# Softmax sums of an attention block: summed and inverted by token on VectorE, turned back by TensorE, scaled out of PSUM on VectorE

## What is computed

```python
scores = jnp.einsum('bqhd,bkhd->bhqk', q, k) / scale      # layer 0 is causal, layer 1 is not
attn = jax.nn.softmax(scores, axis=-1)
out = jnp.einsum('bhqk,bkhd->bqhd', attn, v).reshape(b, s, H * HS)
return out @ W_proj + b_proj
```

## Time and profile before

| what | value |
|---|---|
| median of 3 runs | 792.87 us (792.82 to 799.92) |
| span of the profiled execution, first to last instruction | 785.0 us |
| granted TensorE clock over the span, as a share of full | 0.926 |
| PE busy | 648.3 us, 83% |
| PEld busy | 409.1 us, 52% |
| DVE busy | 533.8 us, 68% |
| ACT busy | 312.7 us, 40% |
| POOL busy | 212.5 us, 27% |

### The profile page before, as it was taken

The page is one execution under the profiler, slowest core; times in us unless marked ns, Lnnn a source line. Parts: engine busy times, 40 slices in busy tenths (PEclk is TensorE's granted clock), DMA queues, the critical chain, the costliest instruction groups (busy, mean ns, idle before and its releaser), DMA issues. The chain is left out here.

```text
span 785.0 us, 9221 instructions
## 1 busy us (share of the span) xinstructions
PE 648.3 (83%) x3406; PEld 409.1 (52%) x3406; DVE 533.8 (68%) x938; ACT 312.7 (40%) x580; POOL 212.5 (27%) x184
## 2 busy tenths in 40 slices
PE   5789677958867889878798879778798899898897
PEld 2234245424323665645265656545266567767597
DVE  2879637769997486668997486668997355543311
ACT  2334112424541325645552325735552324473141
POOL 4559530313562110032443110122543111001100
PEclk8999976979999899999899999989899999999999
DMA  6376910467770002484750002484740000000000
GB/s 123 43 182 157 307 48 1 49 171 167 180 170 1 11 1 24 91 219 110 177 119 10 10 0 26 105 201 108 175 120 10 1 1 2 1 1 11 1 1 10
DMA packets 26642, 61.70 MB, mean 79 GB/s; under 512 B 4928, under 2 KB 12752, under 8 KB 26608
## 3 DMA queue, kind: packets, MB, share of 16 engines
q1 hardware_dynamic: 26608, 61.26, 33.6%
HBM read 53.52 MB, written 3.54 MB: 73 GB/s over the span
## 5 line engine op out<-in xcount | busy, mean ns | idle before, releaser
L1969 POOL TENSOR_TENSOR state<-state,C_rows 128x1024 f32<-128x1024 f32 x42 | 109.6, 2610 | 146.9 <-DVE state L1477 101.4
L1009 PE MATMUL py<-state,sel 128*96 128x512 f32 x168 | 93.2, 688 | 30.6 <-POOL state L1969 30.4
L1082 PE MATMUL pd<-w_dn,act 128*128 128x192 f32 x480 | 85.1, 330 | 3.9 <-ACT act L1849 3.0
L1082 PEld LDWEIGHTS pd<-w_dn,act 128*128 128x128 f32 x480 | 78.6, 191 | 9.4 <-ACT act L1849 4.3
L1009 PEld LDWEIGHTS py<-state,sel 128*96 128x96 f32 x168 | 27.6, 179 | 73.8 <-POOL state L1969 40.3
L1477 DVE TENSOR_TENSOR_SCAN state<-decay,dx_rows 128x512 f32<-128x512 f32 x48 | 64.3, 1380 | 0.8
L919 PE MATMUL py<-identb 128*32 128x512 bf16 x220 | 63.6, 419 | 0.0
L1849 ACT ACTIVATE act<-pu,b_up 128x256 f32<-128x256 f32 x90 | 37.8, 471 | 62.8 <-PE pu L1070 62.4
L1066 PE MATMUL pu<-fT,w_up 128*128 128x256 f32 x180 | 58.3, 406 | 3.7 <-ACT act L1849 3.7
L2018 POOL TENSOR_TENSOR cT<-cT,inv_den 128x256 f32<-128x256 f32 x24 | 18.5, 771 | 144.7 <-DVE inv_den L1694 144.7
L1819 ACT ACTIVATE decay<-d_rows,a_neg 128x255 f32<-128x255 f32 x96 | 40.8, 498 | 29.0 <-DMA d_rows<-delta_dram 28.9
(11 more groups left out here) (298 smaller groups left out, 1288.4 us busy)
## 6 DMA issues: line engine op xcount, KB each, us to landing
dx_rows<-delta_x_dram SPq DMA_DIRECT2D x41, 512.0 KB, 5.1
d_rows<-delta_dram SPq DMA_DIRECT2D x36, 512.0 KB, 6.4
d_rows<-delta_x_dram SPq DMA_DIRECT2D x6, 512.0 KB, 5.2
w_dn<-exp_w_dram SPq DMA_DIRECT2D x1, 2304.0 KB
B_rows<-xdbl SPq DMA_DIRECT2D x4, 512.0 KB, 7.0
C_rows<-xdbl SPq DMA_DIRECT2D x4, 512.0 KB, 10.6
delta_x_dram<-delta_x SPq DMA_DIRECT2D x4, 384.0 KB, 3.4
w_up<-exp_w_dram SPq DMA_DIRECT2D x1, 1536.0 KB
```

The source lines that it names most:

```text
L1009: mm = nc.tensor.matmul(py[0:INNER, :], sel[:, first:first + INNER], flat(states[g % held])[:, paths], start=False, stop=(g == GROUPS - 1) ...
L1082: mm = nc.tensor.matmul(pd[:, WIDTH * tl:WIDTH * (tl + 1)], act[e % 2][:, m, 128 * tl:128 * (tl + 1)], w_dn[:, e, m, :], start=(m == 0), s ...
L1969: nc.gpsimd.tensor_tensor(now, now, C_rows[:, :], ALU.mult).then_inc(sc_done, 1)
```

## The change

The sums are taken by token, inverted as 8 numbers a partition, copied and turned back.

- `sums(ht)` on TensorE stands where `spread(ht)` stood. For each of the two token tiles, `cT[:, ht, 128 tokens]` is the stationary operand and `den_sel[:, :, 0]` (4 columns) the moving one, so that partition = token and column = head.
- `invert_sums(ht)` on VectorE inverts those 128x8 numbers into `inv_tok`, waits for that, and copies each number 32 times into `inv_den` (128x256).
- `spread(ht)` on TensorE turns `inv_den` back with two transposes. It waits for `den_inv`. For ht 0 and 1 it takes the place that `context(2)` and `context(4)` had, and these two move behind `shifted(3)` and `shifted(5)`. They now wait for `ctx_done`.
- `scale_context(ht)` on VectorE multiplies `cT` by `pm[:, 256:512]` in place, after `shift(3)`, after `shift(5)`, and at the end of the layer. GpSimd's `context_scale` is gone.
- A slot "summed" stands between "context" and "spread". No table puts work in it, so in the tail nothing is issued between `sums(2)` and `spread(2)`, and what stands in "spread" comes behind `spread(2)`.

```diff
-SLOTS = [(l, s) for l in range(2) for s in ("turned", "projected", *range(2 * UNITS), "context", "spread",
+SLOTS = [(l, s) for l in range(2) for s in ("turned", "projected", *range(2 * UNITS), "context", "summed",
+                                            "spread",
                                             "output")]
...
                             if u in (2, 4):
-                                pe.wait_ge(den_inv[l], u // 2)
+                                pe.wait_ge(ctx_done[l], u // 2)
...
+                        def sums(ht):
+                            pe.wait_ge(ctx_copied[l], ht + 1)
+                            if ht:
+                                pe.wait_ge(ctx_done[l], ht)
+                            for tl in range(TILES):
+                                mm = nc.tensor.matmul(pm[:, TOKENS + QUAD * tl:TOKENS + QUAD * (tl + 1)],
+                                                      cT[:, ht, 128 * tl:128 * (tl + 1)], den_sel[:, :, 0],
+                                                      start=True, stop=True)
+                            mm.then_inc(den_done[l], 1)
+
                         def spread(ht):
-                            pe.wait_ge(ctx_copied[l], ht + 1)
-                            nc.tensor.matmul(pm[:, TOKENS:2 * TOKENS],
-                                             den_sel[:, :, :].rearrange("p j i -> p (j i)"), cT[:, ht, :],
-                                             start=True, stop=True).then_inc(den_done[l], 1)
+                            pe.wait_ge(den_inv[l], ht + 1)
+                            for tl in range(TILES):
+                                mm = nc.tensor.transpose(pm[:, TOKENS + 128 * tl:TOKENS + 128 * (tl + 1)],
+                                                         inv_den[:, QUAD * tl:QUAD * (tl + 1), :].rearrange("p j i -> p (j i)"),
+                                                         ident[:, :])
+                            mm.then_inc(inv_spread[l], 1)
...
                             row_max(u)
-                            if u >= 1:
+                            if u in (3, 5):
+                                spread(u // 2 - 1)
+                            elif u:
                                 context(u - 1)
                             others((l, 2 * u))
                             shifted(u)
+                            if u in (3, 5):
+                                context(u - 1)
                             if u in (2, 4):
-                                spread(u // 2 - 1)
+                                sums(u // 2 - 1)
                             others((l, 2 * u + 1))
                         context(UNITS - 1)
                         others((l, "context"))
+                        sums(HTILES - 1)
+                        others((l, "summed"))
                         spread(HTILES - 1)
                         others((l, "spread"))
...
                         def invert_sums(ht):
                             dve.wait_ge(den_done[l], ht + 1)
-                            if ht:
-                                dve.wait_ge(ctx_done[l], ht)
-                            nc.vector.reciprocal(inv_den[:, :],
-                                                 pm[:, TOKENS:2 * TOKENS]).then_inc(den_inv[l], 1)
+                            link(nc.vector.reciprocal(inv_tok[:, :], pm[:, TOKENS:TOKENS + TILES * QUAD]))
+                            nc.vector.tensor_copy(inv_den[:, :, :], inv_tok[:, :].unsqueeze(2).to_broadcast(
+                                [128, TILES * QUAD, 2 * HEAD])).then_inc(den_inv[l], 1)
+
+                        def scale_context(ht):
+                            dve.wait_ge(inv_spread[l], ht + 1)
+                            nc.vector.tensor_tensor(cT[:, ht, :], cT[:, ht, :], pm[:, TOKENS:2 * TOKENS],
+                                                    ALU.mult).then_inc(ctx_done[l], 1)
...
                             if u in (2, 4):
                                 context_copy(u // 2 - 1)
+                            if u in (3, 5):
+                                scale_context(u // 2 - 1)
                             others((l, 2 * u))
...
                         invert_sums(HTILES - 1)
+                        others((l, "summed"))
+                        scale_context(HTILES - 1)
                         others((l, "spread"))
...
-                    def context_scale(l, ht):
-
-                        pool.wait_ge(den_inv[l], ht + 1)
-                        nc.gpsimd.tensor_tensor(cT[:, ht, :], cT[:, ht, :], inv_den[:, :],
-                                                ALU.mult).then_inc(ctx_done[l], 1)
-
                     for slot in SLOTS:
                         l, at = slot
-                        if run_a and at in (5, 9, "spread"):
-                            context_scale(l, {5: 0, 9: 1, "spread": 2}[at])
```

More of the change, by code:

```diff
@@ L494, in build @@
         probs = [sb(f"probs{i}", [128, 2, 2, TOKENS]) for i in range(2)]
-        inv_den = sb("inv_den", [128, TOKENS])
+        inv_tok = sb("inv_tok", [128, TILES * QUAD])
+        inv_den = sb("inv_den", [128, TILES * QUAD, HEAD * 2])
         cT = sb("cT", [128, HTILES, TOKENS])
@@ L616, in build @@
         den_inv = [isem(f"sums_inverted{i}") for i in range(2)]
+        inv_spread = [isem(f"inverses_spread{i}") for i in range(2)]
         den_done = [isem(f"sums_spread{i}") for i in range(2)]
```

## The result

The changed kernel takes 826.24 us (median of 4 runs, 821.58 to 831.25), the kernel before 795.62 us beside it: ratio 1.0416, 95% interval 1.0329 to 1.0503. It is slower by 4%, where 804.1 us (792 to 811) was predicted: the sign was right, the size was not.

What follows compares the result with a forecast made beforehand. TensorE's issue order was taken to set the time near the changed tiles, with VectorE counting only where a shift or tail waits. Unit and tail terms summed to +11.2 us: 792.87 + 11.2 = 804.1 us, range 792 to 811.

Steps and rivals of the forecast that it cites:

- The prices: Each new step per tile: reciprocal 0.20 us, copy 0.29, scaling 0.41, two transposes 0.31, sums about 0.5.
- the prediction's reading of the earlier trace: Layer 1: a copy at 0.29 us waits for a running times_C; one at 0.41 us does not.
- The sum: Unit and tail terms of all layers of FIRST, STEADY and LAST added up: +11.2 us in all.
- unit 5 of FIRST's layer 0: Other work fills the slot before shifted, so the cost is the transposes' 0.31 us alone; the sum books 0.6.
- a unit of LAST's layer 1: Nothing in the slot before shifted, so +0.57 us for each of both units; the sum books 0.4 and 0.6.
- The tails: Eight third tiles: TensorE waits inside the chain, 1.6 us from copy to filler against 0.6; +1.0 us where filler is on the path.
- Units 3 and 5: 16 tiles: shorter transposes replace context as cover for the shift; 6.3 us in all by the prediction's terms.
- `shifted(5)` of STEADY's layer 0: A sign in the changed trace: a hole of about 0.4 us before it.
- The clock: Rival: holes and transposes in the eight tails; the clock falls in four, 8 us more, 812 us; chance 0.12.
- the forecast's last sign: The prediction is wrong if the granted clock moves away from 0.926 by more than 0.01.
- The small loss: Rival: TensorE's filler swallows short delays; 798.5 us if half the terms vanish, 796 if only three tails remain; chance 0.36.
- VectorE as the bound: Rival: VectorE's order sets layer 1's units and tails; 13 us faster, 780 us; chance 0.12.

Runs made afterwards that it cites:

- tails_only: The changed kernel with only its tails (third tile of each layer, 8 of 24) new, the other 16 tiles as before; ratio 1.0223 to the kernel before.
- before_pad2: The kernel before with keep_busy matmuls issued as two of 256 columns, 24 in FIRST and all 33 of a STEADY pass; ratio 1.0111.
- before_order: The kernel before with only context(2) and context(4) moved behind shifted(3) and shifted(5); ratio 1.0160.
- before_again: The kernel before, unchanged, run once more for a second trace; 795.36 us.
- after_keep: The changed kernel with 13 more filler matmuls of 512 columns a STEADY pass, in slots 0 to 3 of layer 0; 814.51 us, ratio 1.0298.
- after_keep2: after_keep with three more filler matmuls in each tail of STEADY and LAST, between sums and the transposes; 810.26 us, ratio 1.0218 to the kernel before.
- before_keep: The kernel before with the same 13 filler matmuls in the same slots as after_keep; ratio 1.0012.
- the halves: Two kernels, each with part of the change: only the tails new (ratio 1.0223), or only units 3 and 5 new (ratio 1.0301).
- mm_spread: The changed kernel with the two transposes of the inverses issued as ordinary fp32 matmuls against the identity; ratio 1.0362 to the kernel before.
- before_pad: The kernel before with 26 keep_busy matmuls of a STEADY pass issued as two of 256 columns, FIRST unchanged; ratio 1.0044.
- before_pad3: The kernel before with all 33 keep_busy matmuls of a STEADY pass issued as two of 256 columns, FIRST unchanged; 791.32 us in its one run.

## Why the prediction was wrong

**The prices: right.** Reciprocal 0.20 us, copy 0.29, scaling 0.42, the two transposes 0.22 to 0.37 at full clock (0.22 at 308.00, 0.28 at 438.61) and 0.43 at a clock of 0.50 (496.65), `sums` 0.49 to issue (319.24 to 319.73). The copy is the one that waits for a running `times_C`: at 408.87 it takes 1.32 us and ends at 410.19, with the `times_C` of 407.69 ending 0.15 us before:

```profile
408.87 1.32 DVE L1715 COPY inv_den<-inv_tok 128x256 f32<-128x256 f32 x1
```
```profile
407.69 2.35 POOL L2000 TENSOR_TENSOR state<-state,C_rows 128x1024 f32<-128x1024 f32 x1 [3.54 <-DVE state L1499]
```

That is the prediction's reading of the earlier trace rows, now seen on a copy. The Trainium skill, "SBUF — State Buffer", section "Who interferes with whom", says that a VectorE instruction in a two-port mode and a GpSimd instruction shut each other out, the first one issued going first. The trace agrees with the wait (1.32 us instead of 0.29); that the copy runs in such a mode is not shown.

**The sum: two slips that cancel.** It books 0.6 us for unit 5 of FIRST's layer 0 and 0.4 for a unit of LAST's layer 1, where the list of cases gives 0.3 and 0.6; with these the 11.2 us are 11.0 to 11.1. And the 5.4 us that VectorE stood idle before its reciprocals don't say who waits for them; the rows on the waits do.

**The tails: right.** 1.58 us from the copy to the filler for 1.6, the hole of 0.63 for 0.6, and 5.9 us (3.4) in tails_only for the 4.9 of the sum.

**Units 3 and 5: mechanism right, size too small, by 4.1 us in one fit and within the error in the other.** The moved `context` costs 6.6 us (5.3) by itself and the transposes come on top: 10.4 (7.8) for 6.3. The prediction let the transposes cover part of what `context` had covered, site by site; together the sites gave less cover than that. `shifted(5)` of STEADY's layer 0 waited 0.24 us where 0.4 was forecast, so it isn't that hole; which sites make up the rest wasn't separated.

**The back edge: missed.** No step of the sum looked at the number of instructions. The page counts them and gives the queue that loads them a line of its own, and the change adds 24 matmuls and as many weight loads to TensorE's part of the pass. TensorE starts the second pass 3.3 to 3.9 us late for it, and before_pad2 shows the cost without the change: 3.9 us (2.5).

**The clock: put at nothing in the sum.** This is the step that failed. "In all +11.2 us: the span goes from 785.0 to 796.2" has no term for the clock; it stands only among the rivals, as "If the clock falls once more in four of them, that is 8 us more", with a chance of 0.12. The change moved the mean clock from 0.915 to 0.884, 14 us (15.5). One cold stretch was priced rightly in kind. But the rival looked for it in the eight tails, and about half of the clock that STEADY's layer 0 lost went between 8 and 56 us after its start (0.86 and 0.82 for 0.96), first in units 0 and 1, at holes of 0.9 to 1.6 us that the earlier trace rows could have warned of, since FIRST shows what a hole does; most of the other half went behind 56 us, in unit 5 and the tail. The trace of before ran through that first stretch at 0.96 in both passes, and I took that as a property of the kernel. It was one of several courses of the same code, as before_order's and before_again's two passes show. after_keep, after_keep2 and before_keep show that holes are a condition: where they are filled, the clock stays up. What picks the course in a pass, when the 17.6 us of instructions ahead of it are the same to 0.02 us of busy time, and why the new tails do so every time, the traces don't tell; that stays open.

**The base.** The 7.9 us between the span of 785.0 and the median are not what lies before the first and after the last instruction. In all runs on record that is 1.7 to 1.8 us. The other 6 us lie between the executions: the traced one had a clock of 0.926, where the kernel before has 0.915 on average (35 runs). So the forecast's last sign, a clock more than 0.01 away from 0.926, would have been met by the kernel before itself.

Against the level of the kernel before over all its runs the loss is about 35 us (33): the clock 14 (15.5), the fetch 3.9 (2.5), the order 16.3 (11.2), and 1.3 (4.2) that the halves don't explain. The order is what the prediction summed as 11.2; that the fit in brackets meets this number is no proof of its terms, since it leaves 4.2 us over.

**The other rivals.** The small loss fell: no term vanished. VectorE as the bound fell: it got its 16 us back, and the time rose. The rule of the Trainium skill, "TensorE: Matmul & The Clock Gate", section "Part 4: PE-mode transpose", that transposes don't count as activity for the clock as matmuls do finds no support in mm_spread and isn't excluded by it either.

## What to carry to other kernels

Before pricing a change to a kernel that runs at both levels of the clock, take several traces of it and compare repeated passes of a loop. Where the same instructions run at two clocks, a small hole that an edit opens or moves can cost more by the clock than by its length. Filler matmuls in the old holes, away from the edit, were the one repair here that gave back more than the error, and they did not make up for the change. Count instructions as well as time: a busy engine's loop body can outgrow what is kept of it, and the page's count of instruction packets shows it. When a step becomes a chain through two in-order engines (sums, inverse, turn back, scale), moving its links only moved the wait here, so a long operation that is off the path is better left there.

## What the runs showed of the hardware

- A program that loads its instructions in 20 packets can load 30 when TensorE's code in and ahead of its loop grows, and TensorE then starts the loop's second pass 3.3 to 3.9 us late. A pass of 835 matmuls (before_pad) or 842 (before_pad3) ran without this; one of 833 (the changed kernel) or 842 (before_pad2) did not, with 24 matmuls more in FIRST ahead of it.
- A copy of 128x256 that repeats its input took 0.29 us alone and up to 1.33 beside GpSimd's multiplication.
- Filler matmuls held the clock at 1.00 and 0.96 over the 48 us in which they stood, where the changed kernel without them had 0.86 and 0.82, and did not hold it behind that stretch (0.74 in before_keep's first pass).
- The kernel before scatters from 783.03 to 803.48 us with clocks from 0.895 to 0.930 over 46 runs. The clock explains most of it, 4.5 to 5.5 us for each 0.01, and leaves a scatter of 2.4 us.
